# A 16-head cross attention kernel: the work before the first scores in another order, and two side jobs on other engines or at other places

## The reference, cut to what matters

```python
Q = relu(queries @ Wq + bq)          # queries x: (16, 100, 128)
K = relu(keys @ Wk + bk)             # keys = values = ctx: (16, 1444, 128)
V = relu(values @ Wv + bv)
# 16 heads of width 8
scores = einsum('hbqd,hbkd->hbqk', Qh, Kh) / sqrt(8)
scores = where(sum(keys, -1) == 0, -2**32 + 1, scores)   # key mask
attn = softmax(scores) * (sum(queries, -1) != 0)         # query mask
out = einsum('hbqk,hbkd->hbqd', attn, Vh) + queries
```

## Time and profile before

| what | us |
|---|---|
| median of 3 runs | 408.71 (408.44 to 408.76) |
| the profiled execution | 409.39 |
| its span | 407.6 |
| TensorE busy in the span | 389.7 (96%) |
| ScalarE, VectorE, GpSimd busy | 305.4, 231.0, 14.1 |
| mean granted clock of TensorE, of full | 0.986 |
| the last query ReLU ends | 15.88 |
| SyncE's first query transfer is issued | 15.90 |

### The profile page before, as it was taken

The page is one execution under the profiler, slowest core; times in us unless marked ns, Lnnn a source line. Parts: engine busy times, 40 slices in busy tenths (PEclk is TensorE's granted clock), DMA queues, the critical chain, the costliest instruction groups (busy, mean ns, idle before and its releaser), DMA issues.

```text
span 407.6 us, 13727 instructions
## 1 busy us (share of the span) xinstructions
PE 389.7 (96%) x5216; PEld 265.1 (65%) x5216; DVE 231.0 (57%) x717; ACT 305.4 (75%) x408; POOL 14.1 (3%) x25
## 2 busy tenths in 40 slices
PE   7889699999999999999999999999999988999995
PEld 5756357675767667575767667575766656667663
DVE  1968756473838466473847557473847554366111
ACT  2687548787878787787878787787887864787993
POOL 9400000000000000000000000000000000000000
PEclk9999989999999999999999999999999996999999
DMA  7783616362634526172543616172543615025000
GB/s 238 193 288 154 224 55 238 104 253 87 242 126 163 205 91 238 57 278 73 227 141 149 219 73 242 53 290 78 212 156 136 232 54 226 21 93 209 7 7 8
DMA packets 20960, 62.52 MB, mean 153 GB/s; under 512 B 4938, under 2 KB 10954, under 8 KB 20938
## 3 DMA queue, kind: packets, MB, share of 16 engines
q1 hardware_dynamic: 20218, 61.32, 40.3%
q10 hardware_dynamic: 720, 0.89, 0.7%
HBM read 13.73 MB, written 0.82 MB: 36 GB/s over the span
## 4 chain that ended last, share of the span: by engine, by line
PE 87%; DVE 6%; issue 3%; POOL 2%; ACT 1%; DVEq 0%; ACTq 0%; POOLq 0%
PE psum L523 35%; PE psum L508 26%; PE psum L466 13%; PE psum L461 11%; PE psum L472 2%; POOL selectors L363 2%; DVE k_raw L731 1%; ACT probs L434 1%; DVE k_cent L745 1%; DVE v_biased L767 1%; DVE values L774 1%; DVE k_high L745 1%; DVE q_sum L885 1%; DVE k_parts L899 0%; POOL selectors L356 0%
## 5 line engine op out<-in xcount | busy, mean ns | idle before, releaser
L434 ACT ACTIVATE probs<-psum 128x800 f32<-128x800 f32 x384 | 293.2, 840 | 83.7 <-PE psum L508 83.7
L523 PE MATMUL psum<-probs,values 128*32 128x200 f32 x3072 | 158.5, 340 | 0.7 <-issue 0.7
L508 PEld LDWEIGHTS psum<-query_bd,k_parts 64*128 64x128 f32 x1536 | 97.5, 189 | 48.8 <-ACT probs L434 30.4
L523 PEld LDWEIGHTS psum<-probs,values 128*32 128x32 f32 x3072 | 87.6, 110 | 63.1 <-ACT probs L434 30.4
L508 PE MATMUL psum<-query_bd,k_parts 64*128 64x200 f32 x1536 | 121.5, 289 | 4.7 <-issue 3.0
L731 DVE TENSOR_SCALAR_CACHE_REDUCE k_raw<-psum,bk_sb 128x512 f32<-128x512 f32 (+1 forms) x48 | 34.4, 719 | 85.3 <-PE psum L461 85.2
L466 PE MATMUL psum<-wv_sb,keyT 128*128 128x129 f32 x384 | 59.8, 294 | 0.5 <-DVE v_biased L767 0.5
L461 PE MATMUL psum<-keyT,wk_mixed 128*128 128x512 f32 (+1 forms) x96 | 51.2, 618 | 3.8 <-DVE k_raw L731 3.8
L466 PEld LDWEIGHTS psum<-wv_sb,keyT 128*128 128x128 f32 x384 | 48.2, 193 | 7.3 <-DVE v_biased L767 0.8
L774 DVE TENSOR_SCALAR values<-v_biased,keep 128x128 f32<-128x128 f32 x192 | 43.4, 283 | 6.9
L767 DVE TENSOR_TENSOR v_biased<-psum,bv_sb 128x384 f32<-128x384 f32 x64 | 35.0, 547 | 0.0
(11 more groups left out here) (61 smaller groups left out, 96.6 us busy)
## 6 DMA issues: line engine op xcount, KB each, us to landing
k_parts<-k_high SPq DMA_DIRECT2D x120, 180.5 KB, 2.2
k_parts<-k_low SPq DMA_DIRECT2D x120, 180.5 KB, 2.2
keyT<-in_ctxT SPq DMA_DIRECT2D x15, 722.0 KB, 4.2
query_rep<-k_parts SPq DMA_DIRECT2D x16, 200.0 KB, 2.3
x_sb<-in_x SPq DMA_DIRECT2D x1, 800.0 KB
out<-x_sb SPq DMA_DIRECT2D x16, 50.0 KB
values<-in_xT ACTq DMA_DIRECT2D x1, 600.0 KB, 6.7
keyT<-in_ctxT SPq DMA_DIRECT2D x2, 256.0 KB, 4.0
```

The costliest lines, as they stand in the source:

```text
L434: nc.scalar.activation(probs[:, u % PROB_SLOTS], scores_ps[:, u % SCORE_SLOTS, :, 0:QCOLS], ACT.Exp, scale=SCALE).then_inc(probs_ready, 1)
L508: mm = nc.tensor.matmul(scores_ps[:, u % SCORE_SLOTS, j, n * TCOLS:(n + 1) * TCOLS], k_parts[rows, parity, t, kt * P:(kt + 1) * P], query_ ...
L523: mm = nc.tensor.matmul(o_ps[c * VCOLS:(c + 1) * VCOLS, half * PCOLS:(half + 1) * PCOLS], values[:, parity, kt, half * HALF_PAIRS + c, :], ...
```

## The change

TensorE projects query group 1 ahead of the first queries' selection, and does value groups 0 and 1, selection of chunk 0, value groups 2 and 3, then chunks 1 and 2 by halves (two quads) with scores 0, 1 and 2 between them. Chunks 1 and 2 go through two banks, and ScalarE's last six copies stand behind the exponentials of units 0, 1 and 2. The wait for all twelve copies moves from scores 2 into cycle 0. VectorE reads the first key chunk as soon as it and its bias are there, reads the four value groups (into four buffers) between the parts of `k_low`, and masks them later. q_max moves ahead of batch 1's second key read; `mask_queries` and the sum over the selectors (`sum_heads`) move to the end of `first_batch`. GpSimd rounds the late queries to `q_high` (ScalarE no more does) and makes all of `q_low` but the first 100 columns; the memset of L385 comes after that. In cycles 0 and 1 the side work is placed otherwise.

```diff
-    K_SPREAD_BANKS = (4, 5, 6, 7)
+    K_SPREAD_BANKS = ((4, 5, 6, 7), (6, 7, 6, 7), (6, 7, 6, 7))
+    LATE_SPREADS = {0: ((1, (2, 3)),), 1: ((2, (0, 1)),), 2: ((2, (2, 3)),)}
-        v_biased = sb("v_biased", [P, 2, VGROUP, D])
+        v_biased = sb("v_biased", [P, VGROUPS, VGROUP, D])
...
# SyncE
-            for ready, count, source, slots in ((q_relued, 2 * QGROUPS, q_high, (0, 1)), (q_split, 3, q_low, (2, 3))):
+            sp.wait_ge(q_relued, 2)
+            for ready, count, source, slots in ((q_high_ready, 1, q_high, (0, 1)), (q_split, 3, q_low, (2, 3))):
...
# GpSimd, behind the memset of k_parts' pads
+            relued = queryT[:].rearrange("p (g n) -> p g n", n=QB * SQ)
+            pool.wait_ge(q_relued, 1 + QGROUPS)
+            nc.gpsimd.tensor_copy(q_high[:, 1:QGROUPS, :], relued[:, 1:QGROUPS, :]).then_inc(q_high_ready, 1)
+            for groups, at in ((slice(0, 1), slice(SQ, QB * SQ)), (slice(1, QGROUPS), slice(0, QB * SQ))):
+                if groups.start > 0:
+                    pool.wait_ge(q_high_ready, 1)
+                nc.gpsimd.tensor_tensor(q_low[:, groups, at], relued[:, groups, at],
+                                        q_high[:, groups, at].bitcast(F32), ALU.subtract).then_inc(q_split, 1)
...
# ScalarE
-                for target in (queryT[:, g * QB * SQ:(g + 1) * QB * SQ], q_high[:, g, :]):
+                for target in (queryT[:, g * QB * SQ:(g + 1) * QB * SQ], q_high[:, g, :])[0:2 if g == 0 else 1]:
             relu_queries(0)
+            relu_queries(1)
...
# first queries' spread
-            for g in range(1, QGROUPS):
+            for g in range(2, QGROUPS):
                 relu_queries(g)
+                    if isinstance(b, int) and b == 0 and u in LATE_SPREADS:
+                        for c, quads in LATE_SPREADS[u]:
+                            spread_first(c, quads)
+            spread_first(0, range(QUADS))
+            spread_first(1, (0, 1))
             batch(0, 0)
...
# TensorE, scores()
-                    elif u == EARLY_UNITS:
-                        pe.wait_ge(first_k_spread, KCHUNKS * QUADS)
-            FIRST_SIDE_WORK = (((0, NEXT), (1, NEXT)), ((2, NEXT),), *((step,) for step in VALUES), KEYS[0:2], KEYS[2:])
+            FIRST_SIDE_WORK = (((0, NEXT),), ((1, NEXT), (2, NEXT)), *((step,) for step in VALUES), KEYS[0:2], KEYS[2:])
                     for u in units:
                         next_scores(u + LEAD)
+                    if first and cycle == 0:
+                        pe.wait_ge(first_k_spread, KCHUNKS * QUADS)
...
# TensorE, the opening, behind the key projections
+            pe.wait_ge(xT_loaded, 16)
+            project_queries(1)
...
# selection of the first queries
-            pe.wait_ge(xT_loaded, 16)
-            for g in range(1, QGROUPS):
+            for g in range(2, QGROUPS):
                 project_queries(g)
...
# select_keys(c, quads): waits for first_k_low of chunk c, and for each quad t
-                        pe.wait_ge(first_k_spread, (c - 1) * QUADS + t + 1)
+                        pe.wait_ge(first_k_spread, c * QUADS + t - 1)
...
+            first_values(0)
+            first_values(1)
+            select_keys(0, range(QUADS))
+            first_values(2)
+            first_values(3)
+            select_keys(1, (0, 1))
+            first_scores(0)
+            select_keys(1, (2, 3))
+            first_scores(1)
+            select_keys(2, (0, 1))
+            first_scores(2)
+            select_keys(2, (2, 3))
...
# VectorE, first_batch()
-                for c in range(KCHUNKS):
-                    read_keys(1, c, c)
+                read_keys(1, 0, 0)
+                max_queries()
+                read_keys(1, 1, 1)
+                read_keys(1, 2, 2)
...
-                max_queries()
                 bound_scores(0, 0)
                 bound_scores(1, 1)
-                mask_queries()
...
                 split_keys(2, 0, used + KCHUNKS)
+                mask_queries()
+                sum_heads()
...
# VectorE, the opening, behind the column mixing
-            dve.wait_ge(selecting, 5 + QUADS)
-            v.tensor_reduce(head_sum[:].rearrange("p (t j) -> p t j", t=QUADS),
...
+            dve.wait_ge(bk_loaded, 16)
+            read_keys(0, 0, 0, False)
             dve.wait_ge(q_relued, 2)
-            low_queries(slice(0, 1), slice(0, SQ))
-            dve.wait_ge(bk_loaded, 16)
-            for c in range(KCHUNKS):
+            low_queries()
+            for c in range(1, KCHUNKS):
                 read_keys(0, c, c, False)
...
# maximum, k_high, k_cent
+            low_keys(first_k_low, slice(0, BANK))
+            read_values(0, 0, KCHUNKS, False)
+            read_values(0, 1, KCHUNKS + 1, False)
+            low_keys(first_k_low, slice(BANK, 2 * BANK))
+            read_values(0, 2, KCHUNKS + 2, False)
+            read_values(0, 3, KCHUNKS + 3, False)
+            low_keys(k_low_ready, slice(2 * BANK, SK))
             dve.wait_ge(values_zeroed, 1)
             for g in range(VGROUPS):
-                finish_values(0, 0, g, KCHUNKS + g, False)
+                mask_values(0, 0, g, KCHUNKS + g, False)
```

More of the change, by code:

```diff
@@ L185, in attention @@
         q_relued = sem("q_relued")
+        q_high_ready = sem("q_high_ready")
         q_split = sem("q_split")
@@ L631, in _, with first_values @@
             mm.then_inc(first_q_selected, 1)
-            pe.wait_ge(xT_loaded, 16)
-            for g in range(1, QGROUPS):
+            for g in range(2, QGROUPS):
                 project_queries(g)
-            pe.wait_ge(wv_loaded, 32)
-            pe.wait_ge(pads_zeroed, 2)
-            pe.wait_ge(q_relued, 2)
-            for g in range(VGROUPS):
+            def first_values(g):
                 if g > 0:
@@ L757, in bound_scores, with read_values @@
                                 ).then_inc(bound_made, 1)
-            def finish_values(b, parity, g, index, before=True):
-                rows = slice(g * VGROUP, (g + 1) * VGROUP)
+            def read_values(b, g, index, before=True):
                 filled, free, bank = (work_filled, work_free, work_ps) if before else \
@@ L765, in finish_values, with mask_values @@
                 work = bank[:, 0:VGROUP * VW].rearrange("p (n w) -> p n w", w=VW)
-                v.tensor_scalar(keep[:, rows], work[:, :, D], 0.0, None, ALU.not_equal).then_inc(keep_ready, 1)
-                v.tensor_tensor(v_biased[:, g % 2], work[:, :, 0:D],
+                v.tensor_scalar(keep[:, g * VGROUP:(g + 1) * VGROUP], work[:, :, D], 0.0, None, ALU.not_equal
+                                ).then_inc(keep_ready, 1)
+                v.tensor_tensor(v_biased[:, g], work[:, :, 0:D],
                                 bv_sb[:].unsqueeze(1).to_broadcast([P, VGROUP, D]), ALU.add
                                 ).then_inc(free, 1)
+            def mask_values(b, parity, g, index, before=True):
                 dve.wait_ge(keep_ready, VGROUPS * b + g + 1)
-                dve.wait_ge(free, index + 1)
+                dve.wait_ge(work_free if before else first_evacuated, index + 1)
                 for n in range(VGROUP):
@@ L894, in max_queries, with low_queries, sum_heads @@
                 dve.wait_ge(q_masked, 1)
-            def low_queries(groups, at):
-                relued = queryT[:].rearrange("p (g n) -> p g n", n=QB * SQ)
-                v.tensor_tensor(q_low[:, groups, at], relued[:, groups, at], q_high[:, groups, at].bitcast(F32),
-                                ALU.subtract).then_inc(q_split, 1)
+            def low_queries():
+                v.tensor_tensor(q_low[:, 0, 0:SQ], queryT[:, 0:SQ], q_high[:, 0, 0:SQ].bitcast(F32), ALU.subtract
+                                ).then_inc(q_split, 1)
+            def sum_heads():
+                dve.wait_ge(selecting, 5 + QUADS)
+                v.tensor_reduce(head_sum[:].rearrange("p (t j) -> p t j", t=QUADS),
+                                selectors[:, :, Q_HIGH, :, 0].bitcast(F32).rearrange("p t (j d) -> p t j d", d=DH),
+                                AX.X, ALU.add).then_inc(selectors_ready, 1)
             def mix_columns(target, source, done):
@@ L911, in _ @@
             mix_columns(wk_mixed, wk_sb, wk_permuted)
-            dve.wait_ge(selecting, 5 + QUADS)
-            v.tensor_reduce(head_sum[:].rearrange("p (t j) -> p t j", t=QUADS),
-                            selectors[:, :, Q_HIGH, :, 0].bitcast(F32).rearrange("p t (j d) -> p t j d", d=DH),
-                            AX.X, ALU.add).then_inc(selectors_ready, 1)
+            dve.wait_ge(bk_loaded, 16)
+            read_keys(0, 0, 0, False)
             dve.wait_ge(q_relued, 2)
-            low_queries(slice(0, 1), slice(0, SQ))
-            dve.wait_ge(bk_loaded, 16)
-            for c in range(KCHUNKS):
+            low_queries()
+            for c in range(1, KCHUNKS):
                 read_keys(0, c, c, False)
```

30 lines of the change are left out of this document (15 added, 15 removed).

## The result

Slower. The changed kernel takes 415.1 us in the median (412.6 to 416.3, 4 executions), the kernel before on the same chip 408.57 (408.16 to 408.76): a ratio of 1.0152 (95% interval 1.0111 to 1.0192). The forecast was 413.8 us, in a range of 406.2 to 416. Medians and ranges here are over all executions; the ratios leave out those that took over 1.5% longer than the fastest of their kernel, which are one in experiment 9 and two in experiment 11.

What follows compares the result with a forecast made beforehand. TensorE, with no idle entry in the steady part, was taken as the bound, so early losses stay. +3.05 + 1.6 + 1.4 - 0.9 = +5.15 us on 409.39 gave 414.5, on the median's scale 413.8 us, range 406.2 to 416.

Steps and rivals of the forecast that it cites:

- First key read and q_low: Opening, VectorE: key read at 8.05, q_low's subtraction held by affine_select until 10.25, k_high issued at 12.0, ended at 14.40.
- GpSimd's three instructions: Opening: GpSimd's query copy 1.3 us and two q_low subtractions 0.6 and 2.4, together 4.3 us, until 18.7.
- If GpSimd keeps the port over its joints: Opening: k_cent waits behind all three GpSimd instructions, first key selection at 20.3 instead of 17.25, +3.05 us; chance 0.40.
- rival 1: Opening: GpSimd and VectorE take turns, first key selection at 17.8, +2.65 us in all, total 411.4; chance 0.20.
- From the first selection to C2: First key selection to batch 0's third cycle (C2): ScalarE sets the pace, 16.7 us against 15.27, +1.4; lower clock +1.6 separately.
- Change of batch: First change of batch: stall moves from a key projection to a value product, wait 3.5 us, clock 1.6, net -0.9 us.
- Rival 2: Opening: affine_select doesn't hold q_low's subtraction, k_high precedes the memset, first key selection 14.4, -2.35 us, total 406.4; chance 0.24.
- the fork: Opening: q_low's first subtraction inside affine_select costs 0.2 us if it passes, 1.5 if it waits; the forecast took waiting.

Runs made afterwards that it cites:

- experiment 9: Changed kernel with three more VectorE memsets in the opening: 411.14 us (405.93 to 413.05), ratio 1.0024 to the kernel before.
- experiment 11: Changed kernel run once more, unedited: 414.86 us (408.62 to 416.07), ratio 1.0072 to the kernel before; its profiled execution took 408.62.
- experiment 7: Changed kernel with the first part of q_low made after the second and third key read: 409.53 us, ratio 1.0017 to the kernel before.
- experiment 6: Kernel before with GpSimd waiting for k_cent before the memset of values and what follows: 408.04 us, ratio 0.9981 to the kernel before.
- experiment 3: Changed kernel with the head sums between batch 2's first and second key read, q_sum and mask between second and third: 410.79 us, ratio 1.0054.
- experiment 4: Changed kernel with ten short VectorE memsets to an unread tile added in the opening: 410.57 us, ratio 1.0044 to the kernel before.
- experiment 1: Changed kernel with value groups 2 and 3 projected ahead of the selection of key chunk 0: 413.09 us, ratio 1.0120 to the kernel before.
- experiment 12: Changed kernel with the key bias transfer as SyncE's second issue instead of ScalarE's fourth: 415.85 us, ratio 1.0158 to the kernel before.
- experiment 2: Changed kernel with GpSimd waiting for k_cent before the memset of values and all that follows: 410.63 us, ratio 1.0055 to the kernel before.
- experiment 8: Kernel before with only q_max, q_sum and the mask moved, the sum over the selectors left: 408.06 us, ratio 0.9996 to the kernel before.
- experiment 5: Changed kernel with the edits of experiment 2, experiment 3 and experiment 4 together: 402.03 us, ratio 0.9857 to the kernel before.
- experiment 10: Changed kernel with the edits of experiment 5 and experiment 7, and value groups 2 and 3 behind scores 0: 402.92 us, ratio 0.9867.

## Why the prediction was right, and where it was wrong

The total came out 1.3 us from the forecast, and that is luck in good part: one term of the sum is 2.8 us too large, a loss of 3.95 us is not in it at all, and the two nearly cancel. By the profiles the terms are +0.23, +2.93 (1.4 and 1.6 were forecast), -1.04 and +3.95, together +6.07 against 5.15.

- **First key read and q_low: right.** Read at 8.08 (8.05 forecast); the subtraction held under the last affine_select, 8.75 to 10.02 (10.25 forecast; affine_select ends at 10.06); `k_high` issued at 11.69 and ended at 14.40 (12.0 and 14.40). Experiments 7 and 11 show the other branch: 0.26 us. The Trainium skill, "SBUF — State Buffer", section "SBUF: two separate sides", had the rule that a VectorE instruction with two SBUF inputs is shut out by a GpSimd instruction reading SBUF; the trace now agrees, with 1.27 us against 0.26. Alone `k_high` takes 0.97 us, not the 0.76 that the forecast named: 0.76 is what is left behind a GpSimd instruction, and the sum used it rightly. A memset, which reads nothing, did not hold `k_low`'s subtraction of the same kind in experiment 6 (three chunks in 1.80 us from 14.95).
- **GpSimd's three instructions: right in size.** 1.04 + 0.66 + 2.64 = 4.34 us against 4.3. The Trainium skill's "GPSIMD Engine Reference", section 3.1, gives 2.2 ns an element for a two-input add, and the trace agrees.
- **"If GpSimd keeps the port over its joints": wrong.** That step put `k_cent` behind all three, and the first selection at 20.3; it was the branch with the largest chance, 0.40. `k_cent` got in behind the copy, and the selection came at 17.48, by rival 1 at 17.8. The term was +3.05 and is +0.23. I had generalised from one row, the copy that lost every joint near 3 us, and weighed two alternations less. The joints are not kept by one side: between the two memsets near 12.98 VectorE lost in the changed kernel and in experiments 3 and 4, and won in 1 and 12. What settles one isn't shown here.
- **From the first selection to C2: right.** 18.20 us against 16.7 plus 1.6 for the clock; lost clock 0.52 + 1.00 + 0.20 = 1.7 us from the windows of 18 to 24. Without a clock loss it is 16.6 (experiment 2). Key chunk 2 is 0.45 us late, against 0.4.
- **Change of batch: right.** The wait is 3.52 us (3.5 forecast), by q_sum's 2.28, the head sums' 0.38 and the mask in front of the copy; the clock lost 1.00 + 0.68 = 1.7; the difference is -1.04 against -0.9. Experiments 3 and 8 each show where the wait comes from.
- **Not in the sum: +3.95 us at batch 14.** VectorE stands 2.79 us, TensorE for it 2.23, and 0.72 + 0.98 = 1.7 us of clock follow. It was in all seven profiles of kernels with the changed kernel's number of VectorE instructions (the changed one and experiments 1, 2, 3, 7, 11, 12), and a pause of that size was in none with three or ten more, or with the list of before (experiments 4, 5, 6, 8, 9, 10 and the kernel before). The profile shows no semaphore that it waits for. The clock behind the wait varies: 1.7 us here, 3.4 in experiment 3 and nothing in experiment 1. The transfers around it: in the changed kernel one packet of the DMA queue that carries instructions (q14) falls in the window of 367.5 to 369, while VectorE already stands; in the kernel before one is seen at 361.9 to 363, while `k_cent` runs, and the copy at 364.47 has no pause. The rows are that queue's packets, MB and share in each window (first after, then before), and VectorE before:

```profile
q14 instruction: 1, 0.01, 1.3%
```

```profile
q14 instruction: 1, 0.01, 3.0%
```

```profile
364.20 0.35 DVE L819 SCALAR_TENSOR_TENSOR x_sb<-o_norm,q_mask,x_sb 100x128 f32<-100x128 f32 x1 [0.28 <-DVE o_norm L813]
364.47 0.57 DVE L798 COPY o_sb<-psum 128x400 f32<-128x400 f32 x1
```

Experiments 4 and 9 show that the pause goes with a few added instructions, though the shift of the tiles went with them. That it is a fetch of the next piece of the list, which comes late where nothing covers it, is what the packets suggest. With the windows narrowed to 0.1 us, the first of the two late q14 packets falls near 367.6 in the changed kernel, and the copy starts 1.8 us behind it; in the other six profiles with the pause it is 1.8 us too. In experiment 9 the packet is at 358.8, and the instruction behind the gap of 0.21 starts 1.7 us later; in the kernel before it is at 362.3, and the instruction behind a gap of 0.28 starts at 364.20, 1.9 us later. In experiments 4, 5 and 10 it comes 8.7 to 8.8 us ahead of the copy, where VectorE waits for TensorE anyway. Which engine a packet served isn't recorded, so the fetch is argued and not shown.

**The rivals.** Rival 1 (turns) is what happened at the joints, and alone would have given 411.4. Rival 2 was no less real: it happened in experiment 11, in one of four executions, and cost the forecast nothing only since the slower course is the usual one. It gave C2 at 30.60 and an execution of 408.62; less the late loss of 3.95, which it also had (the clock was 0.50 at 364 to 366), that is near 404.7, against 406.4 in the forecast. Experiment 9's profiled execution is this chain without the late pause, and it took 405.93.

**The spread.** Behind the same wait of 3.52 us the lower clock cost 1.7 us in the changed kernel, 4.5 in experiment 4 (windows summed from 60 us on) and 3.0 in experiment 2. A second place of this kind is the exit of the batch loop, near 340 us: TensorE stands 2.3 to 3.1 us there in all fourteen profiles. The clock lost behind that wait was 3.4 us in those of the changed kernel and the kernel before, so their difference is free of it, but 1.7 in eight others and nothing in experiment 1. The executions of one kernel lay 2.4 to 7.5 us apart in all experiments but the tenth (0.5). Those of the kernel before lay 0.6 apart beside the result, but 2.5 to 3.2 in the larger groups beside the experiments. The clock and, in the changed kernel, the fork are in this spread; their shares weren't measured, and one profiled execution against another is best compared at C2 and at single waits, not by the total.

## What to carry to other kernels

Before giving GpSimd a side job, list the VectorE instructions issued beside it, their kind and inputs, and which of them leads to the critical path; keep GpSimd out until those are done with a semaphore (one line, 4.0 to 4.5 us here, where the job itself had the time to come later). Work moved out of one wait goes in front of another reader on the same in-order engine: look who waits for the instruction behind the new place. When a loss shows up far from the edit and "issue" is all that stands before it, shift the engine's instructions by a few idle ones before looking for a cause in the data, and look at what the instruction queues moved at that time.

## What was not expected of the hardware

- The joint between two back-to-back GpSimd instructions is won by either side, and differently in kernels with the same instructions there: `k_high` issued near 11.7 to 11.9 ended at 14.40 or near 13.8.
- A VectorE pause of 2.79 us without any releaser, moved or hidden by 3 to 10 short instructions elsewhere (ten took 0.19 us in all).
- The lower clock behind one and the same TensorE wait (3.52 us) cost between 1.7 and 4.5 us.
- Some 0.2 us (the subtraction issued at 8.43 or at 8.59) decide whether it takes 0.26 or 1.46 us, and with that, in the changed kernel, over 5.1 us at C2 (30.60 or 35.68).
